# A transformer decoder layer on one core: the first norm scaled on ScalarE, the two best experts found for all rows at once, and the context products made in f16 parts

## What is computed

```python
x = x + linear_attention(layernorm(x), W)                 # q, k: elu + 1; state k^T v, rows divided by q.sum(k)
x = x + cross_attention(layernorm(x), ctx, Wq, bq, Wk, bk, Wv, bv)   # softmax over the 77 rows of ctx
h = layernorm(x)
logits = h @ Wr                                            # 8 experts
topk_p, topk_i = top_k(softmax(logits), 2); topk_p /= topk_p.sum()
x = x + ffn_shared(h) + sum_over_the_two(topk_p * ffn_expert[topk_i](h))   # 256 -> 1024 -> 256, tanh gelu
```

## Time and profile before

| | us |
|---|---|
| median of 3 runs (lowest, highest) | 941.33 (940.8, 943.58) |
| the profiled execution, its own time | 941.67 |
| its span, first to last instruction | 939.9 |
| PE busy | 801.1 (85%) |
| DVE busy | 631.3 (67%) |
| ACT busy | 356.6 (38%) |
| POOL busy | 236.3 (25%) |

### The profile page before, as it was taken

How to read it: one execution, slowest core, us unless ns; L and a number is a source line. 1 busy time by engine, 2 the same in 40 slices (tenths; PEclk the granted TensorE clock), 3 DMA queues, 4 the chain that set the end, 5 groups by cost and what they waited for, 6 DMA issues and landing times.

```text
span 939.9 us, 21652 instructions
## 1 busy us (share of the span) xinstructions
PE 801.1 (85%) x6791; PEld 673.8 (72%) x6791; DVE 631.3 (67%) x2006; ACT 356.6 (38%) x777; POOL 236.3 (25%) x221
## 2 busy tenths in 40 slices
PE   3999999998569610199999999999999999999995
PEld 2666766666358400088888888888888888888884
DVE  4579888988579400088888666666666666666663
ACT  4554554454244200045555333333333333333331
POOL 2211011101100677400000133333333333333333
PEclk9899999999579855589999999999999999999998
DMA  5556666853334523245555343435534444443440
GB/s 164 146 151 176 132 174 170 186 123 83 57 109 157 186 106 110 92 127 167 167 151 173 63 69 54 64 59 62 62 61 64 65 65 63 63 65 65 62 55 7
DMA packets 168045, 98.07 MB, mean 104 GB/s; under 512 B 110316, under 2 KB 163336, under 8 KB 167944
## 3 DMA queue, kind: packets, MB, share of 16 engines
q1 hardware_dynamic: 153640, 79.65, 34.4%
q0 software_dynamic: 14304, 17.10, 10.6%
HBM read 37.84 MB, written 37.88 MB: 81 GB/s over the span
## 4 chain that ended last, share of the span: by engine, by line
PE 60%; issue 20%; another core or an unknown queue 8%; DVE 6%; DMA 2%; ACT 1%; POOL 1%; SPq 1%; POOLq 0%; DVEq 0%; ACTq 0%
PE bank_st L1163 10%; PE bank_kv L1175 10%; PE bank_st L1161 10%; PE bank_kv L1177 10%; PE bank_st L1162 10%; PE bank_kv L1176 10%; DMA stage_w<-in_L_ffn_Wfc_s 1%; POOL rstd L518 1%; DVE w_parts L959 1%; DVE expert_buffers L971 1%; DVE w_parts L738 0%; DMA expert_buffers<-rows_by_expert 0%; DVE expert_buffers L972 0%; DVE stats L827 0%
## 5 line engine op out<-in xcount | busy, mean ns | idle before, releaser
L695 ACT ACTIVATE expert_buffers<-bank_st,bias_columns 128x256 f32<-128x256 f32 x440 | 208.5, 474 | 422.8 <-DVE expert_buffers L972 218.9
L971 DVE TENSOR_SCALAR expert_buffers<-expert_buffers 128x256 f16<-128x256 f32 x440 | 128.8, 293 | 199.4 <-ACT expert_buffers L695 127.2
L1175 PE MATMUL bank_kv<-w_parts,expert_buffers 128*128 (+1 forms) x880 | 241.4, 274 | 1.7 <-DVE expert_buffers L972 1.7
L1177 PE MATMUL bank_kv<-w_parts,expert_buffers 128*128 (+1 forms) x880 | 241.3, 274 | 0.0
L1176 PE MATMUL bank_kv<-w_parts,expert_buffers 128*128 (+1 forms) x880 | 241.3, 274 | 0.0
L972 DVE SCALAR_TENSOR_TENSOR expert_buffers<-expert_buffers 128x256 f16<-128x256 f32 x440 | 188.3, 428 | 15.1
L1161 PE MATMUL bank_st<-expert_buffers,w_parts 128*128 128x256 f16 x624 | 170.1, 273 | 1.4 <-DMA expert_buffers<-rows_by_expert 1.4
L1162 PE MATMUL bank_st<-expert_buffers,w_parts 128*128 128x256 f16 x624 | 170.1, 273 | 0.0
L1163 PE MATMUL bank_st<-expert_buffers,w_parts 128*128 128x256 f16 x624 | 170.1, 273 | 0.0
L1161 PE MATMUL bank_st<-w_parts 128*128 128x256 f16 x256 | 71.9, 281 | 73.2 <-issue 51.3
L561 POOL DMA_INDIRECT out<-expert_buffers,token x78 | 121.8, 1561 | 20.6 <-issue 20.3
(11 more groups left out here) (150 smaller groups left out, 1061.4 us busy)
## 6 DMA issues: line engine op xcount, KB each, us to landing
rows_by_expert<-w_parts SPq DMA_DIRECT2D x13, 795.0 KB, 5.5
stage_w<-in_L_ffn_Wfc SPq DMA_DIRECT2D x16, 512.0 KB
stage_w<-in_L_ffn_Wproj SPq DMA_DIRECT2D x16, 512.0 KB
expert_buffers<-in_L_ffn_bproj SPq DMA_DIRECT2D x39, 128.0 KB
rows<-in_x SPq DMA_DIRECT2D x16, 256.0 KB, 3.3
x_residual<-rows SPq DMA_DIRECT2D x16, 256.0 KB, 4.7
expert_buffers<-x_residual SPq DMA_DIRECT2D x16, 256.0 KB
out<-expert_buffers SPq DMA_DIRECT2D x16, 256.0 KB
```

Of the source, the lines that this page charges most:

```text
L695: act.activation(g32[f % 2], hid[f % 2][:, 0:BLK], ACT.Gelu_apprx_tanh, bias=bias, scale=UNSCALE).then_inc(s["gelu_done"], 1)
L971: chain(dve.tensor_scalar(g[:, 0, :], g32[f % 2], A_SCALE, None, ALU.mult), "g_hi", c + 1)
L1175: pe.matmul(y, g[:, 0, tile(t)], w_hi, start=f == 0 and t == 0, stop=False, skip_group_check=True)
L1177: op = pe.matmul(y, g[:, 1, tile(t)], w_hi, start=False, stop=f == FC - 1, skip_group_check=True)
```

## The change

1. **First norm.** For batches 1 to 15 the scaling of norm 1 moves from DVE to ACT: DVE makes `shift = -mean * rstd` (128x2), and ACT `x * rstd + shift` in two instructions of 128x256 with scale and bias read from SBUF (`norm_first`), just ahead of the high part of norm 1.
2. **Logits.** The logits of all 32 tiles stay in bank 6. The copy of logits and the search (L744, L777 to L783) leave the steps. `top_two` finds the two best with compares and reductions over many tiles: for batches 0 to 14 in step 19, for batch 15 in step 20. Its results are the masks `hot[0]`, `hot[1]` themselves, which the routing made before in two instructions of 128x256 (L871).
3. **Context.** It is turned in bank 6, right behind the scores and ahead of `kv`; ACT copies a high f16 part ahead of the exponentials, DVE makes the low part; the products with `fold`, the bias column and Wv take three f16 matmuls for each f32 one. The weights are split once in step 1.

The diff, cut to its core:

```diff
+TOP_STEPS = {19: range(0, 15), 20: range(15, 16)}
@@ banks
-        ctxT_ps = bank7[:, 0:DK * CK].rearrange("p (k n) -> p k n", k=DK)
+        ctxT_ps = bank6[:, 256:256 + DK * CK].rearrange("p (k n) -> p k n", k=DK)
-        lg_ps = bank6[:, 0:TB * E].rearrange("p (t n) -> p t n", t=TB)
+        lg_ps = bank6[:, 0:TILES * E].rearrange("p (t n) -> p t n", t=TILES)
@@ GpSimd
+            pool.iota(below_i, [[1, E]], base=-E, channel_multiplier=0).then_inc(s["below_set"], 1)
@@ ScalarE
+            def norm_first(b):
+                act.wait_ge(s["shift_ready"], b)
+                got(act, "lo1_ready", b - 1)
+                for t in range(TB):
+                    op = act.activation(xn[0][:, t, :], rows[:, b * TB + t, 0:D], ACT.Identity,
+                                        bias=shift[:, t:t + 1], scale=rstd[:, t:t + 1])
+                op.then_inc(s["xn1_ready"], 1)
...
                 if live(i - 2):
                     high(1, i - 2)
+                if live(i - 2):
+                    got(act, "ctxT_done", i - 2)
+                    copy(ctxT16[:, :, 0, :], ctxT_ps, "ctxT_hi")
...
                 if live(i + 1) and not (isinstance(i, int) and i == -1):
+                    norm_first(i + 1)
                     high(0, i + 1)
...
-                if live(i - 2):
-                    got(act, "ctxT_done", i - 2)
-                    copy(ctxT, ctxT_ps, "ctxT_copied")
@@ ScalarE, step 1 (the low parts are made by VectorE at the end of step 1)
+                    act.activation(fold16[:, :, 0, :], fold_ps, ACT.Copy, scale=A_SCALE).then_inc(s["fold_hi"], 1)
+                    act.wait_ge(s["wkT_done"], 1)
+                    act.activation(wv16[:, :, 0, :], wv, ACT.Copy, scale=W_SCALE).then_inc(s["wv_hi"], 1)
@@ VectorE
+            def top_two(batches):
...
+                got(dve, "logits_done", batches[-1])
...
+                count_top(dve.tensor_scalar(values, lg_ps[:, ts, :], UNSCALE, None, ALU.mult))
+                count_top(dve.tensor_reduce(top[:, 0, ts], values, AX.X, ALU.max))
+                for j, out_hot in enumerate((best, second)):
+                    count_top(dve.tensor_tensor(part, values, of(j), ALU.is_equal))
+                    count_top(dve.tensor_tensor(part, part, below, ALU.mult))
+                    count_top(dve.tensor_reduce(at, part, AX.X, ALU.min))
+                    count_top(dve.tensor_tensor(out_hot, below, at_e, ALU.is_equal))
+                    if j == 0:
+                        count_top(dve.scalar_tensor_tensor(values, best, -3.0e38, values, ALU.mult, ALU.add))
+                        count_top(dve.tensor_reduce(top[:, 1, ts], values, AX.X, ALU.max))
...
-                for n, b in ((1, i - 2), (2, i - 4), (0, i + 1)):
+                elif live(i + 1):
+                    dve.scalar_tensor_tensor(shift[:, :], mv[:, 0, :, 0], -1.0, rstd[:, 0:TB], ALU.mult, ALU.mult)\
+                        .then_inc(s["shift_ready"], 1)
+                for n, b in ((1, i - 2), (2, i - 4)):
...
+                if i in TOP_STEPS:
+                    top_two(TOP_STEPS[i])
+                if live(i - 2):
+                    got(dve, "ctxT_hi", i - 2)
+                    dve.tensor_tensor(ctxT16[:, :, 1, :], ctxT_ps, ctxT16[:, :, 0, :], ALU.subtract)\
+                        .then_inc(s["ctxT_lo"], 1)
@@ VectorE, routing
-            for j in range(2):
-                op = dve.tensor_tensor(hot[j], iota_te, top_f[:, :, j:j + 1].broadcast_to([P, TILES, E]), ALU.is_equal)
@@ TensorE, behind the scores
+                if live(i - 2):
+                    b = i - 2
+                    pe.wait_ge(s["ctx_loaded"], (b + 1) * 16)
+                    if b == 0:
+                        pe.wait_ge(s["fold_ready"], 1)
+                    for k in range(DK):
+                        op = pe.transpose(ctxT_ps[:, k, :], ctx_sb[0:CK, tile(k)], ident[0:CK, 0:CK])
+                    op.then_inc(s["ctxT_done"], 1)
...
-                            pe.matmul(k2T_ps[:, m, :], fold[:, k, tile(m)], ctxT[:, k, :], start=k == 0, stop=k == DK - 1)
+                            for a, c in PASSES:
+                                pe.matmul(k2T_ps[:, m, :], fold16[:, k, a, tile(m)], ctxT16[:, k, c, :],
...
+                    if b == TOP_STEPS[20][0]:
+                        pe.wait_ge(s["top_step"], 2)
```

More of the change, by code:

```diff
@@ L106, in decoder_layer @@
         rstd = sb("rstd", [P, 3 * TB], F32)
+        shift = sb("shift", [P, TB], F32)
         nmax = sb("nmax", [P, TB], F32)
@@ L112, in decoder_layer @@
         zinv = sb("z_inv", [P, TB], F32)
-        lg = sb("logits", [P, TB, E], F32)
-        max8 = sb("max8", [P, TB, 8], F32)
-        max8_at = sb("max8_at", [P, TB, 8], U32)
-        top = sb("top_values", [P, TILES, 2], F32)
-        top_f = sb("top_experts", [P, TILES, 2], F32)
+        top = sb("top_values", [P, 2, TILES], F32)
         dest = sb("dest_rows", [P, 2, TILES], I32)
@@ L158, in decoder_layer @@
         proj16 = lend(DK * 3 * D).bitcast(F16).rearrange("p (k l n) -> p k l n", k=DK, l=2)
-        fold = lend(DK * D, "p (k n) -> p k n", k=DK)
-        wk = lend(DK * D, "p (k n) -> p k n", k=DK)
+        fold16 = lend(DK * D).bitcast(F16).rearrange("p (k l n) -> p k l n", k=DK, l=2)
+        wk32 = lend(DK * D)
+        wk = wk32.rearrange("p (k n) -> p k n", k=DK)
+        wv16 = wk32.bitcast(F16).rearrange("p (k l n) -> p k l n", k=DK, l=2)
+        row16_cols = lend(DK).bitcast(F16).rearrange("p (k l) -> p k l", k=DK)
         wv = lend(DK * D, "p (k n) -> p k n", k=DK)
@@ L211, in decoder_layer @@
         picked = scratch(TE).bitcast(F16)[:, 0:TE]
-        iota_te = te(scratch(TE))
-        iota_i = scratch(TE).bitcast(I32)
+        logits = te(scratch(TE))
+        place_at = scratch(TILES)
+        below_i = scratch(E).bitcast(I32)
+        below_e = scratch(E)
         dlog = scratch(TILES)
@@ L709, in _ @@
             route_count = [0]
+            top_count = [0]
             def chain(op, name, count, own=False):
@@ L739, in split_w2, with of @@
                                          w2[:, ds(half * 2048, 1024)], ALU.mult, ALU.subtract).then_inc(s["w2_lo"], 1)
+            def top_two(batches):
+                ts = slice(batches[0] * TB, (batches[-1] + 1) * TB)
+                n = (batches[-1] + 1 - batches[0]) * TB
+                values, best, second, part = logits[:, ts, :], hot[0][:, ts, :], hot[1][:, ts, :], chosen[:, ts, :]
+                at, at_e = place_at[:, ts], place_at[:, ts].rearrange("p (t a) -> p t a", a=1).broadcast_to([P, n, E])
+                below = below_e[:, :].rearrange("p (a e) -> p a e", a=1).broadcast_to([P, n, E])
+                def of(j):
+                    return top[:, j, ts].rearrange("p (t a) -> p t a", a=1).broadcast_to([P, n, E])
+                got(dve, "logits_done", batches[-1])
+                if batches[0] == 0:
+                    dve.wait_ge(s["below_set"], 1)
+                    count_top(dve.tensor_copy(below_e, below_i))
+                count_top(dve.tensor_scalar(values, lg_ps[:, ts, :], UNSCALE, None, ALU.mult))
[8 more added lines that the diff above has]
+                        count_top(dve.tensor_reduce(top[:, 1, ts], values, AX.X, ALU.max))
@@ L771, in step @@
                         .then_inc(s["lo3_ready"], 1)
-                if live(i - 5):
-                    b = i - 5
-                    apart(dve)
-                    got(dve, "logits_copied", b)
-                    for t in range(TB):
-                        op = dve.max(max8[:, t, :], lg[:, t, :])
-                    chain(op, "max_step", b + 1, own=True)
-                    for t in range(TB):
-                        op = dve.max_index(max8_at[:, t, :], max8[:, t, :], lg[:, t, :])
-                    chain(op, "top_step", b + 1)
-                    dve.tensor_copy(top[:, ds(b * TB, TB), :], max8[:, :, 0:2])
-                    dve.tensor_copy(top_f[:, ds(b * TB, TB), :], max8_at[:, :, 0:2]).then_inc(s["top_ready"], 1)
+                if i in TOP_STEPS:
[4 more added lines that the diff above has]
+                        .then_inc(s["ctxT_lo"], 1)
                 if (half := half_of(i)) is not None:
@@ L863, in over_e @@
                 return ap.rearrange("p (t a) -> p t a", a=1).broadcast_to([P, TILES, E])
[L865 to L868 removed]
+            then(dve.tensor_tensor(dlog, top[:, 1, :], top[:, 0, :], ALU.subtract))
+            dve.wait_ge(s["route_iota"], 3)
             then(dve.tensor_copy(iota_blk, iota_blk_i))
[L870 to L872 removed]
             dve.tensor_tensor(picked.rearrange("p (t e) -> p t e", e=E), hot[0], hot[1], ALU.add)\
@@ L1097, in step @@
                     op.then_inc(s["attn_done"], 1)
-                if live(i - 2):
-                    b = i - 2
-                    pe.wait_ge(s["ctx_loaded"], (b + 1) * 16)
-                    got_if(pe, "pT_copied", b - 1)
-                    if isinstance(b, int) and b == 0:
-                        pe.wait_ge(s["fold_ready"], 1)
-                    for k in range(DK):
```

(2 more changed lines are left out.)

60 lines of the change are left out of this document (34 added, 26 removed).

## The result

| | us |
|---|---|
| before, in the same session (lowest, highest of 4) | 941.07 (939.73, 943.58) |
| after (lowest, highest of 4) | 984.61 (982.36, 988.62) |
| ratio, 95% interval | 1.0468 [1.0440, 1.0495] |
| predicted | 960, range 947 to 975 |
| after, profiled execution: own time, span | 988.62, 986.9 |

The change makes the kernel slower, and by more than the range allowed. The profiled execution is the slowest of the four, 4.0 us above their median; its span grew by 986.9 - 939.9 = 47.0 us. Nearly all of it arises before the second part: the first gelu starts at 315.37 instead of 268.47, 46.9 later. So the steps are the place to look, and the busy time of two steps side by side shows at once what the forecast left out. The columns are as in the earlier trace rows; the rows are steps 8, 9 and 10, each from one start of the scores to the next.

The account below looks back on a forecast made before the run. VectorE and TensorE were nearly full, VectorE later; ScalarE's scalings would delay the low part of norm 1. 14.3 + 3.6 + 0.3 - 1.5 + 2.0 = +18.7 on 941.67 gave 960 us, range 947 to 975.

Parts of the forecast that it names:

- the steady step: Steps 3 to 14: low part of norm 1 starts 1.19 us later, period 14.7 us, +14.3 us in all.
- the pair: The two norm 1 scalings on ScalarE, behind the copy of pT: 0.61 us each, 1.13 us together with the wait.
- all at full granted clock: Steady step before the change: period 13.54 us, with TensorE busy 12.40, VectorE 11.96 and ScalarE 6.71 at full clock.
- rival 2: TensorE's clock falls in the longer gap ahead of the scores: 1.4 x 12 us on top, 977; chance 0.11.
- The f16 products: Context products in steady steps: save TensorE about half a microsecond, but it already waited for VectorE; no gain counted.
- The context's load: Needed earlier, ahead of kv: 0 in steady steps, up to 1.3 a step for the range; +3.6 us in step 2.
- just in time: In steady steps the context's load lands when TensorE wants it, 4.5 us after issue: cost 0.
- rival 1: The context is late in each steady step too, each of 12 steps 0.8 us longer: 970; chance 0.15.
- The tail: Search in step 19 and after: 0.9 us sticks out, chained operations take 2.5 us, first gelu later: +2.0 us.
- The last steps: Step 15: turning ahead of kv, +0.3 us; step 17: f16 context products and moved turning, -1.5 us.

Follow-up runs that it names:

- e2: The kernel before with part 1 alone (first norm scaled on ScalarE): 954.06 us, ratio 1.0146.
- e1: The changed kernel with ten unused matmuls on TensorE ahead of the scores in steps 3 to 15: 974.08 us, ratio 1.0378.
- e5: The kernel before with one unused reduction on VectorE right ahead of the v2 addition in steps 3 to 15: 957.51 us, ratio 1.0199.
- e6: The kernel before with two unused reductions on VectorE right ahead of the v2 addition in steps 3 to 15: 979.21 us, ratio 1.0426.
- e4: The kernel before with parts 2 and 3, without part 1: 968.75 us, ratio 1.0297.
- e10: The changed kernel with the norm pair ahead of the high part of norm 2 on ScalarE: 884.49 us, ratio 1.0206 to the kernel before on its chip.
- e11: e8 with high part of norm 1 ahead of ScalarE's kv operations, low part ahead of kfeat, q behind pv, qfeat behind v2: 882.76 us, ratio 1.0193.
- e7: The kernel before with parts 2 and 3 and ten unused matmuls ahead of the scores in steps 3 to 15: 953.62 us, ratio 1.0151.
- e9: e7 with the context's load on SyncE ahead of the load of x and the padding store: 871.68 us, ratio 1.0070 on another chip.
- e8: The kernel before with parts 1 and 2, norm pair ahead of the high part of norm 2 on ScalarE: 942.39 us, ratio 1.0020.

## Why the prediction was wrong

- **Direction and the steady step: right.** Period 14.88 and 14.69 in the two steps with full clock (forecast 14.7), VectorE idle 1.78 us ahead of the low part (1.7), the pair and the high part behind it 1.11 us apart in start (1.13). One such operation has a mean of 593 ns (forecast 0.61 us); two in a row take 1.08. The estimate of 585 ns from the Trainium skill, "ScalarE: Activation LUTs", section "What ACT_TABLE_LOAD costs", with two pointer operands, agrees with the trace within 10 ns. Alone, the term is 0.90 a step (e2), since there `kv` isn't behind the turning of the context.
- **The step that failed: "all at full granted clock" was carried over to the longer wait.** The forecast gave rival 2 a chance of 0.11 and argued against it that dense f32 work stands ahead of the gap. That argument fell: in all of these kernels the eight state matmuls (1.98 us) end right ahead of the wait, and the clock falls all the same. e1 shows the cost, 16.9 us in steps 4 to 14 of the profiled executions; e5 and e6 show that a longer wait is enough. The rival's price was near: 1.4 us, measured 1.69 where `kv` takes 4.44; the scores are not hit, but some two thirds of `kv` are (at the lower level throughout it takes 5.3). It struck in 10 of the 12 steps 3 to 14.
- **The f16 products, costed at nothing, had a price.** "The f16 products save TensorE about half a microsecond, but it already waited for VectorE, and now waits longer." That longer wait was the price. Without part 3, part 1 leaves the wait at 1.38 and the clock held (e2); without part 1, part 3 makes it 2.04 and the clock falls (e4). The wait was read there as slack.
- **The context's load: its term mis-sized.** Step 2 lost 6.1 us instead of 3.6, since `kv` not only waited 2.56 us but then took 5.33. Step 3 lost 5.7 instead of 1.2: another 1.38 of wait, and the low clock. In steps 4 to 14 "just in time" held as long as the steps were long: late once, by 0.24. With shorter steps it is late in 6 of 11, by 0.2 to 0.4 in e1 and by 0.25 to 1.34 in e4. This is rival 1, mostly under its price of 0.8.
- **The tail: right.** Twelve operations of 240 columns at 0.44 and twelve of 16 columns at 0.21 (forecast 0.44 and 0.21), first gelu +1.9 (forecast +2.0):

```profile
305.84 0.41 DVE L773 TENSOR_SCALAR w_parts<-bank 128x240 f32<-128x240 f32 x1
306.28 0.40 DVE L774 TENSOR_REDUCE top_values<-w_parts 128x30 f32<-128x240 f32 x1
...
311.12 0.17 DVE L773 TENSOR_SCALAR w_parts<-bank 128x16 f32<-128x16 f32 x1
311.33 0.17 DVE L774 TENSOR_REDUCE top_values<-w_parts 128x2 f32<-128x16 f32 x1
```

- **The last steps.** Step 17 gained 1.7 (forecast 1.5). Step 15 lost 1.5 instead of 0.3, of which 0.9 is its `kv` at 3.67 us; step 16, costed at nothing, lost 1.5 as well. That is the clock too: the granted clock of the step is 0.86, against 1.00 before, while e4 and e10 keep 1.00 in it and take 10.34 and 10.33 us, like the 10.41 before.

With the clock mended by e1 in steps 4 to 14, the profiled execution is 25.9 us above that of before, against 18.7 forecast. Of the 7.2 between, 6.3 are steps 2 and 3 (11.1 in e1 against 4.8) and 1.9 steps 4 to 14; steps 15 to 17 add 0.9 and what follows them gives back 1.8. e1 was the fastest of its four, so the agreement owes something to the choice of the execution. What is not explained is why, with the same wait, one step falls and the next does not (e6, e11), why 1.37 us ahead of the products is enough in e11 where 1.38 ahead of the scores is not in e2, and why e4 falls in 8 of the 11 steps and e10 in 4. These two ran on different chips, and TensorE waits for the context longer in e4 (up to 1.34 us) than in e10 (up to 0.39); nothing here tells the causes apart.

## What to carry to other kernels

A wait of TensorE is not free room: when an edit lengthens it (by a slower neighbour, or by making TensorE's own work shorter), price the long matmul groups behind it at the lower clock as well, from a row at that level, and give this a real chance even if dense work stands ahead of the wait. Giving work from the busiest engine to an idle one helps only where the idle one is idle and the busy one is waited for; here the same pair cost 0.90 us a step behind `kv` and nothing ahead of it, and the relief bought less than 0.1 us a step (13.46 against 13.54). When a consumer is moved ahead of its old place, look at the step in which the load has the least lead, not only at the steady one.

## What the runs showed that was not expected

- With the wait ahead of the scores the clock fell after 1.92 us in 4 of 11 steps, after 2.77 in 9, and in none after 1.38. With a wait of 1.37 us at another place, ahead of the products (e11), it fell in 4 of 11. Ten matmuls of 512 columns (2.32 us) put into the wait ahead of the scores held it in the profiled executions of e1, e7 and e9.
- The chips differ in the shared blocks. While the rows are scattered (82 to 86 us), TensorE is busy 21 to 27% of the time in the traces of before, after and the first eight runs, and 99% in the later ones. The stretch 340 to 360 us, e8 and then e9, with a scatter on GpSimd in both:

```profile
340.00:360.00 20.00, 1.03 (x6) 0.43 (x5) 0.05 (x1) 0.47 (x1) 15.27 (x16) 0.50 0.40 135
```
```profile
340.00:360.00 20.00, 19.91 (x180) 16.84 (x178) 17.58 (x45) 10.23 (x18) 15.70 (x15) 1.00 0.86 264
```

  DMA moves 135 GB/s in the one and 264 in the other, and the kernel before takes 941 and 865 us. e8 and e9 differ in their steps, not in this part of the code, and the kernel before differs by as much; the cause is open.
